# A two-layer gated attention and expert block: row transposes moved from TensorE to transposing transfers, and the batches interleaved in a new order

## The chip, the cores and the metric

The kernel runs on one core of one Trainium2 chip. The metric is the device time of one execution in microseconds (us), taken as the median of the runs. A core has a matmul engine (TensorE, PE in the profile, with its weight loads as PEld), three elementwise engines (VectorE or DVE, ScalarE or ACT, GpSimd or POOL), and SyncE (SP), which here only issues DMA transfers. Each engine works through its own list of instructions strictly in order and waits on semaphores that the other engines and the transfers raise.

## The reference, cut to what matters

The input is 32 batches of 256 tokens by 256 features, with 77 context rows a batch. Four residual steps follow each other, all of them on a layer norm of x:

```
x = x + tanh(g_xattn[0]) * L0_xattn(norm(x), ctx)   # relu projections, relu scores, mask, relu output
x = x + tanh(g_ffn[0])   * L0_ffn(norm(x))          # [x,-x] @ (+-1) 512x1024, relu, (+-1) 1024x1024, relu, (+-1) 1024x256
x = x + tanh(g_xattn[1]) * L1_xattn(norm(x), ctx)   # argmax of 77 scores picks memory rows; 16 heads, softmax over 77*; projection
x = x + tanh(g_ffn[1])   * L1_ffn(norm(x))          # 64 experts, 8 per token, capacity 128, and a shared expert
```

(*) In the kernel a memory row that is picked several times is one key with a count, so a token has 16 heads of 77 logits, 1232 probabilities in all, of which one row group (128 tokens, 8 heads) holds 616, padded to 640.

The layer norm and the softmax run along a token's row, while a matmul contracts over the partitions. So a norm (256 tokens by 256) has to be turned before the next projection, and so have the probabilities and the attention's output. Products that need more than 16 bits are split: a value is written as a high half in f16 and a low half (value minus high half, f16), and the matmul runs over both.

## The kernel before, in words

One batch is a chain of four stages, named in the code by the first letter of its steps: a (first attention), b (binary feed-forward: `b_l0`, `b_l1`, `b_l2`), c (second attention) and d (shared expert and routing). A hand-written `body(n)` on each engine interleaves them: it runs b of batch n, c of batch n-1, d of batch n-2 and a of batch n+1. The orders of the five engines are written out separately, and agree only by semaphores. Bodies 3 to 30 are a hardware loop, the others stand apart in front of and behind it. After all batches comes the expert phase: POOL has scattered every token's row into a table by expert (`scatter`, L647), SP loads 64 blocks of it (`load_rows`), and PE runs the experts.

**Turning a norm on PE.** ACT writes the norm in f32 (`ln_norm`, L817). PE transposes it by four 128x128 f32 transposes into PSUM (`transposes`, L1113, and `c_att`, L1294, for the attention's output). ACT copies the high half from PSUM (`tr_high`, L825) and DVE subtracts for the low half (`tr_low`, L1655). Norms 1, 2, 3 and the attention's output go this way: 16 transposes a batch. The four row groups of probabilities take five blocks each (`c_pt`, L1262 on PE, L896 on ACT, L1751 on DVE), 20 a batch.

**Turning a norm on SP.** Norm 0 already takes another way in all batches but the first two. POOL computes norm 0 and both halves as rows in f16, and one transposing DMA on SP (`turn_x`, L416) turns eight 128x128 f16 blocks from SBUF to SBUF.

**The feed-forward on PE.** `b_l0` (L1173) has four pieces of eight matmuls, into two PSUM banks in turn; piece j waits until piece j-2 was evicted, by ACT (`h_h`, L862) and then DVE (`h_l`, L1677). `b_l1` (L1189) has eight pieces of 16, `b_l2` (L1205) two of 16. DVE then adds the residual (`b_x2`, L1691), takes the statistics (L1626 to L1639), POOL the root (L690), DVE the shift (L1644), and ACT the norm.

**Other queues.** POOL copies x1 aside (`keep_x1`, L685) so that `x1` comes free. SP also loads x and the context, passes rows to the table's staging tile (`pass_rows`, L424), stores x4 and copies the queries into the stacked tile (`stack`, L430 and L433, eight transfers a batch). Near the end it loads the held weights of every fourth expert (`load_held`, 16 transfers of 384 KB).

## Time and profile before

| | |
|---|---|
| median of 2 runs | 1716.07 us (1713.07 and 1719.07) |
| span of the profiled execution | 1753.8 us |
| PE busy | 1618.4 us, 92% |
| DVE, ACT, POOL busy | 1345.8, 1049.5 and 1023.1 us |
| DMA in the whole span | 117.41 MB, 67 GB/s |

The profile follows one execution, and that one was longer than the timed runs: its span stands 37.7 us above the median. Differences are therefore worked out inside the profiled span and then set against the median. Busy shares are averages over set-up, the loop, the last batches and the expert phase; what a change in the loop is worth is read from windows inside it. A PE clock of 1.00 in a window means the higher of TensorE's two levels (2.4 GHz), 0.50 the lower one (1.2 GHz).

### The profile page before, as it was taken

How to read it: one execution, taken by the hardware profiler on the slowest of the kernel's cores; microseconds unless marked ns; L12 is line 12 of the kernel's file. 1: busy time of each engine (PE TensorE's matmuls, PEld its weight loads, DVE VectorE, ACT ScalarE, POOL GpSimd, SP SyncE). 2: the span in 40 equal slices, each digit the busy share in tenths (PEclk: the TensorE clock that was granted, in tenths of full speed). 3: DMA queues.
4: the chain of work that ended last, by engine and by line, in shares of the span. 5: the costliest groups of instructions: out<-in, count | busy, mean ns of one | idle time of the engine just before them, and what ended most of it. 6: DMA issues, size and time to landing. Idle time of an engine off the chain costs nothing.

```text
span 1753.8 us, 51499 instructions
## 1 busy us (share of the span) xinstructions
PE 1618.4 (92%) x16676; PEld 1417.6 (81%) x16676; DVE 1345.8 (77%) x4739; ACT 1049.5 (60%) x2917; POOL 1023.1 (58%) x1664
## 2 busy tenths in 40 slices
PE   5799999999999999999999999999999997578885
PEld 3688888888888888888888888888888886367774
DVE  6488888888788888888888888888888875546554
ACT  3466666666666666666666666666666654334442
POOL 4124666666566666666666666666666654455544
PEclk8899999999999999999999999999999998689998
DMA  7502211121111111111111111111111122258886
GB/s 225 170 22 65 59 55 52 55 58 46 34 37 36 45 33 52 37 28 38 41 37 37 37 33 33 33 34 37 29 37 33 31 63 78 94 126 204 188 198 126
DMA packets 146627, 117.41 MB, mean 67 GB/s; under 512 B 74656, under 2 KB 136042, under 8 KB 146585
## 3 DMA queue, kind: packets, MB, share of 16 engines
q1 hardware_dynamic: 112792, 97.71, 19.8%
q0 software_dynamic: 33792, 19.17, 6.2%
q8 instruction: 22, 0.36, 0.1%
q14 instruction: 21, 0.16, 0.0%
HBM read 51.63 MB, written 111.84 MB: 93 GB/s over the span
## 4 chain that ended last, share of the span: by engine, by line
PE 73%; DMA 9%; issue 6%; ACT 5%; DVE 4%; POOL 3%; another core or an unknown queue 1%; POOLq 0%; SPq 0%; ACTq 0%; DVEq 0%
PE bank L1189 21%; DMA out<-ey,aid 9%; PE bank L1087 9%; PE bank L1173 7%; PE ps_yo L1205 5%; PE ps_yo L1087 4%; PE ps_m L1087 4%; PE ps_lg L1087 4%; ACT p L890 3%; PE ps_tr L1113 3%; PE ps_yo L1262 2%; PE ps_m L1285 2%; PE ps_pt L1262 2%; PE ps_pt L1087 2%; PE ps_lg L1249 2%
## 5 line engine op out<-in xcount | busy, mean ns | idle before, releaser
L647 POOL DMA_INDIRECT table<-xs,slot x496 | 505.3, 1019 | 188.7 <-issue 168.6
L890 ACT ACTIVATE p<-ps_lg,rmax 128x77 f32<-128x77 f32 x1024 | 251.6, 347 | 78.9 <-DVE rmax L1745 78.3
L1189 PE MATMUL bank<-h_h,held 128*128 128x256 f16 x2048 | 266.6, 273 | 2.1 <-DVE h_l L1677 1.9
L1189 PE MATMUL bank<-h_l,held 128*128 128x256 f16 x2048 | 266.3, 273 | 0.0
L602 POOL TENSOR_TENSOR pool_pad<-pad_in 128x1 f32<-128x1 f32 x418 | 90.4, 216 | 284.2 <-PE ps_tr L1294 116.8
L1189 PEld LDWEIGHTS bank<-h_l,held 128*128 128x128 f16 x2048 | 200.8, 98 | 23.6
L1189 PEld LDWEIGHTS bank<-h_h,held 128*128 128x128 f16 x2048 | 195.3, 98 | 24.3 <-issue 1.8
L1677 DVE SCALAR_TENSOR_TENSOR h_l<-bank,h_h 128x512 f16<-128x512 f32 x256 | 173.0, 685 | 32.2 <-ACT h_h L867 13.8
L690 POOL TENSOR_TENSOR rs<-nt,minushalf 128x2 f32<-128x2 f32 x128 | 93.2, 728 | 126.1 <-DVE nt L1639 115.2
L867 ACT ACTIVATE h_h<-bank 128x512 f16<-128x512 f32 x128 | 77.1, 602 | 130.3 <-PE bank L1189 127.1
L784 POOL DMA_INDIRECT out<-ey,aid x64 | 98.6, 1541 | 96.7 <-DVE aid L2031 64.1
L1745 DVE TENSOR_REDUCE rmax<-ps_lg 128x4 f32<-128x308 f32 x256 | 119.2, 476 | 40.2 <-PE ps_lg L1249 32.5
L862 ACT ACTIVATE h_h<-bank 128x512 f16<-128x512 f32 x128 | 76.4, 597 | 86.6 <-PE bank L1173 85.5
L1205 PE MATMUL ps_yo<-held,h_h 128*128 128x256 f16 x512 | 117.4, 275 | 0.1
L1205 PE MATMUL ps_yo<-held,h_l 128*128 128x256 f16 x512 | 117.1, 272 | 0.0
L1173 PE MATMUL bank<-xt_h,held 128*128 128x256 f16 x512 | 100.2, 278 | 8.4 <-DVE dn_l L1571 5.9
L1626 DVE BATCH_NORM_STATS2 stats<-x 128x6 f32<-128x256 f32 x256 | 96.4, 418 | 10.9 <-DMA x<-in_x 0.7
L1087 PE MATMUL bank<-xt_h,gu_h 128*128 128x256 f16 x512 | 99.1, 276 | 5.5 <-DVE ac L1835 5.4
L1173 PE MATMUL bank<-xt_l,held 128*128 128x256 f16 x512 | 99.9, 277 | 0.0
L1087 PE MATMUL bank<-xt_l,gu_h 128*128 128x256 f16 x512 | 99.0, 276 | 0.0
L1087 PE MATMUL bank<-xt_h,gu_l 128*128 128x256 f16 x512 | 99.0, 276 | 0.0
L817 ACT ACTIVATE xn<-x,nb,rs 128x256 f32<-128x256 f32 x128 | 69.5, 591 | 39.2 <-DVE nb L1644 38.4
(275 smaller groups left out, 4520.2 us busy)
## 6 DMA issues: line engine op xcount, KB each, us to landing
ew<-in_e_wts SPq DMA_DIRECT2D x48, 384.0 KB
table<-xg SPq DMA_DIRECT2D x8, 1284.0 KB, 17.8
xg<-table SPq DMA_DIRECT2D x64, 160.5 KB
xs<-xr SPq DMA_DIRECT2D x31, 320.0 KB
x<-in_x SPq DMA_DIRECT2D x32, 256.0 KB
out<-x SPq DMA_DIRECT2D x32, 256.0 KB
table<-xs,slot POOLq DMA_INDIRECT x496
held<-in_e_wts SPq DMA_DIRECT2D x16, 384.0 KB
```

The lines of the kernel that those rows point to most:

```text
L602: return g.tensor_tensor(pool_pad[:, site:site + 1], pad_in[:, :], pad_in[:, :], ALU.mult)
L647: return g.indirect_dma_start(out=table, out_offset=bass.IndirectOffsetOnAxis(ap=slots[:, t, k:k + 1], axis=0), in_=rows[:, t, :], in_offs ...
L690: g.tensor_tensor(rs[i][:, :], nt[i][:, 0, :], minushalf[:, :], ALU.pow).then_inc(ln_root[i], 1)
L784: g.indirect_dma_start(out=out, out_offset=bass.IndirectOffsetOnAxis(ap=aid[u][:, 0:1], axis=0), in_=ey[u][:, :], in_offset=None, bounds_c ...
L890: ins = a.activation(p32[r % 2][:, h * S2:(h + 1) * S2], ps_lg[:, g_, h % HB * S2:(h % HB + 1) * S2], ACT.Exp, bias=rmax[r % 2][:, h:h + 1])
L1087: ins = mm(out_, s_, m_, start=(start and i == 0), stop=(stop and i == len(seq) - 1))
L1173: ins = mm(two(bank[j % 2])[:, m % 2, :], s_, m_, start=(k == 0), stop=(k == 3))
L1189: ins = mm(two(bank[j % 2])[:, m % 2, :], wb1[:, k, m * P:(m + 1) * P], hp[:, k, :], start=(i == 0 and k == 0), stop=(i == 1 and k == FK - 1))
L1205: ins = mm(two(ps_yo)[:, t, :], hp[:, k, t * P:(t + 1) * P], wb2[:, k, :], start=(i == 0 and k == 0), stop=(i == 1 and k == FK - 1))
L1626: last = v.bn_stats(stats[i][:, t, :], src[:, t, :])
L1677: v.scalar_tensor_tensor(hl[:, 2 * j:2 * j + 2, :], two(bank[j % 2]), 0.0, hh[:, 2 * j:2 * j + 2, :], ALU.max, ALU.subtract).then_inc(lo.s ...
L1745: v.tensor_reduce(rmax[r % 2][:, g_ * HB:(g_ + 1) * HB], ps_lg[:, g_, 0:HB * S2].rearrange("p (h k) -> p h k", k=S2), AX, ALU.max, negate= ...
```

## The change

**The turns.** All 36 transposes a batch leave PE. ACT now writes the high half of a norm or of the attention's output from the f32 rows into an f16 row tile (`high`), DVE the low half beside it (`low`), and SP turns both at once by a transposing DMA of eight blocks (`turn(i)`, i = 1 to 4) into the tile that the matmuls read. Probabilities go the same way in tiles of ten blocks (`c_phi` on ACT, `c_plo` on DVE, `turn_p(r)` on SP, r = 0 to 3). So SP issues eight more transposing DMAs a batch, beside the one of norm 0. Only the first two norms 0 stay on PE.

**PSUM and SBUF.** The tile that held turned probabilities now takes the a-stage; routing and its counts share another; the queries of the second attention go into `ps_yo`. The product tile `ac` has two buffers in place of four, and tiles of the expert phase lie over the loop's h tiles. POOL copies x2 aside as well (`keep_x2`, 128x512), and its scatters lose the waits that paced them.

**The order.** `body(n)` now spans four batches: `b_l0` and pieces 0 to 3 of `b_l1` of n, the rest of the feed-forward and the start of c of n-1, the rest of c and the start of d of n-2, the end of d of n-3. Three bodies (NB to NB+2) drain the pipeline.

The first place is the end of the feed-forward on PE. `ps_yo` is the output of `b_l2`, `bank` the two alternating banks, `ps_m<-vb,pt` the attention's values, `ps_m<-wc` its projection. Before, at the end of the loop body and its head:

```order
L1087 MATMUL bank<-xt_h,gu_l 128x256 x2
L1113 MATMUL ps_tr<-ident,xn 128x128 x2
...
L1173 MATMUL bank<-xt_h,held 128x256 x2
L1173 MATMUL bank<-xt_l,held 128x256 x2
...
L1087 MATMUL ps_m<-xt_h,wp_h 128x256 x2
```

With the change:

```order
L1257 MATMUL ps_yo<-held,h_l 128x256
...
L1326 MATMUL ps_m<-vb,pt 128x34 x3
L1326 MATMUL ps_m<-vb,pt 128x51 x3
...
L1223 MATMUL bank<-xt,held 128x256 x16
L1223 MATMUL bank<-xt,held 128x256 x8
...
L1149 MATMUL ps_m<-wc_h,xt 128x256 x2
...
L1149 MATMUL ps_yo<-xt,wp_h 128x256 x4
...
L1241 MATMUL bank<-h_h,held 128x256 x8
```

Before, pieces of the shared expert (`gu`) stood between the end of `b_l2` and the first `b_l0` of the next batch. Now only the last two row groups of the values stand there, and all four pieces of `b_l0` follow in one run.

The second place is ACT's list around the eviction of `b_l0` (`h_h<-bank`). Before, at the end of the body and its head:

```order
L817 ACTIVATE xn<-x,nb,rs 128x256 x2
L923 ACTIVATE ac_h<-ac 128x256
...
L918 ACTIVATE th<-bank 128x256
...
L825 ACTIVATE xt_h<-ps_tr 128x512
...
L862 ACTIVATE h_h<-bank 128x512
...
L871 ACTIVATE qp_h<-ps_m 128x512
```

With the change:

```order
L908 ACTIVATE rows_hl<-att 128x512
L894 ACTIVATE xn<-x,nb,rs 128x256 x2
L908 ACTIVATE rows_hl<-xn 128x512
L946 ACTIVATE h_h<-bank 128x512 x4
L955 ACTIVATE qp_h<-ps_yo 128x512
L894 ACTIVATE xr<-x,nb,rs 128x256 x2
L908 ACTIVATE rows_hl<-xr 128x512
L951 ACTIVATE h_h<-bank 128x512
```

The four evictions of `b_l0` now follow the high half of the attention's output and the whole of norm 2, which is made from the x2 that `b_l2` has just delivered.

The third place is SP's list. Before, one turn of the loop, and behind the last batch the end of the queue:

```order
L430 DMA qst<-qp_h 32x512 x4
L433 DMA qst<-qp_l 32x512 x4
L439 DMA out<-x 128x2x256
L416 DMA_TRANSPOSE xt<-xh 128x8x128
...
L424 DMA xs_z<-xr 128x2x320
L501 DMA held<-in_e_wts 128x768 x4
L531 DMA xg<-table 128x321 x2
L439 DMA out<-x 128x2x256
```

With the change:

```order
L470 DMA_TRANSPOSE pt<-p_hl 128x10x128
...
L497 DMA out<-x 128x2x256
...
L459 DMA_TRANSPOSE xt<-rows_hl 128x8x128 x3
...
L487 DMA qst<-qp_h 32x512 x4
L490 DMA qst<-qp_l 32x512 x4
L459 DMA_TRANSPOSE xt<-rows_hl 128x8x128
...
L481 DMA xs_z<-xr 128x2x320
L497 DMA out<-x 128x2x256
L572 DMA held<-in_e_wts 128x768 x4
L600 DMA xg<-table 128x321 x5
```

The store of the last batch (`out<-x`) and the last four held weights now both stand ahead of the first rows of the table (`xg<-table`).

The diff, cut to the new functions and the lines that set the order:

```diff
+            def turn(i, b):            # SP
...
+                sp.wait_ge(lo_ok[i], made)
...
+                sp.dma_start_transpose(xt[i][:, :, :, :, :].rearrange("p a t c n -> p (a t c) n"),
+                                       rows_hl[i][:, :, :, :].rearrange("p a t d -> p (a t d)")).then_inc(turned[i], 16)
+            def turn_p(r, b):          # SP
...
+                sp.dma_start_transpose(pt[r % 2][:, :, :, :].rearrange("p a k n -> p (a k) n"),
+                                       p_hl[r % 2][:, :, :].rearrange("p a n -> p (a n)")).then_inc(pt_in[r % 2], 16)
+            def high(i, b, src):       # ACT
...
+                w(act, turned[i], 16 * b)
+                a.activation(rows_hl[i][:, 0], src, ACT.Copy).then_inc(hi_ok[i], 1)
+            def c_phi(r, b):           # ACT
...
+                a.activation(p_hl[r % 2][:, 0, :], p32[r % 2][:, :], ACT.Copy).then_inc(p_hi.sem, 1)
+            def low(i, b, src):        # DVE
+                dve.wait_ge(hi_ok[i], b + 1)
+                v.tensor_tensor(rows_hl[i][:, 1], src, rows_hl[i][:, 0], ALU.subtract).then_inc(lo_ok[i], 1)
# SP, body(n), the second half
+                    store_x4(d)
+                    turn(1, m)
+                    turn(4, c)
+                    turn(2, n)
+                    stack(n)
+                    turn(3, c)
# PE, body(n), around b_l2
+                    c_av(1, d)
+                    b_l2(0, c)
+                    b_l2(1, c)
+                    c_av(2, d)
+                    c_av(3, d)
+                    b_l0(0, n)
...
+                    b_l0(3, n)
+                    c_wc(d)
+                    c_qp(c)
+                    b_l1(0, n)
# ACT, body(n), its head
+                    high(4, d, att[:, :, :])
+                    ln_norm(2, c, x2, xn[2])
+                    high(2, c, xn[2][:, :, :])
+                    b_l0(0, n)
...
# DVE, body(n), around b_x2
+                    low(1, n, xn[1][:, :, :])
+                    b_x2(c)
+                    c_norm(2, d)
+                    ln_sums(2, c, x2, x2_ok)
+                    ln_moments(2, c)
+                    c_norm(3, d)
+                    ln_shift(2, c)
+                    low(4, d, att[:, :, :])
+                    low(2, c, xn[2][:, :, :])
+                    b_l0(0, n)
```

(Conditions such as `if on(d):`, which drop a step where its batch does not exist, are left out between the lines.)

## Rows read from the trace of the kernel before

**Rows 1.** The page: span, and busy time, share and instructions of each engine.

```profile
span 1753.8 us, 51499 instructions
...
PE 1618.4 (92%) x16676; PEld 1417.6 (81%) x16676; DVE 1345.8 (77%) x4739; ACT 1049.5 (60%) x2917; POOL 1023.1 (58%) x1664
```

**Rows 2.** Windows, in the loop: us, busy by engine, PE clock, DMA share, GB/s.

```profile
375.00:420.00 45.00, 44.80 (x492) 39.72 (x491) 38.00 (x134) 29.88 (x84) 29.11 (x51) 1.00 0.20 58
```

**Rows 3.** Timeline of PE in the loop: start, length, instruction.

```profile
704.94 0.38 PE L1173 MATMUL bank<-xt_h,held 128*128 128x256 f16 x2
...
748.07 0.60 PE L1113 MATMUL ps_tr<-ident,xn 128*128 128x128 f32 x4
748.51 0.38 PE L1087 MATMUL bank<-xt_h,gu_h 128*128 128x256 f16 x2
...
749.82 0.38 PE L1173 MATMUL bank<-xt_h,held 128*128 128x256 f16 x2
...
750.69 0.38 PE L1087 MATMUL ps_m<-xt_h,wp_h 128*128 128x256 f16 x2
```

**Rows 4.** Timeline from the end of `b_l2` to norm 2.

```profile
743.34 0.38 PE L1087 MATMUL bank<-xt_h,gu_h 128*128 128x256 f16 x2
...
743.64 0.75 DVE L1691 SCALAR_TENSOR_TENSOR x<-ps_yo,sc,x_kept 128x512 f32<-128x512 f32 x1 [0.32 <-PE ps_yo L1205]
...
744.49 0.75 DVE L1626 BATCH_NORM_STATS2 stats<-x 128x6 f32<-128x256 f32 x2
...
745.89 0.72 POOL L690 TENSOR_TENSOR rs<-nt,minushalf 128x2 f32<-128x2 f32 x1 [0.27 <-issue]
...
746.64 0.16 DVE L1644 TENSOR_TENSOR nb<-nt,rs 128x2 f32<-128x2 f32 x1
...
746.87 1.08 ACT L817 ACTIVATE xn<-x,nb,rs 128x256 f32<-128x256 f32 x2
```

**Rows 5.** Lines of DVE, 300 to 1,200 us: busy, mean ns, idle before.

```profile
L1677 DVE SCALAR_TENSOR_TENSOR h_l<-bank,h_h 128x512 f16<-128x512 f32 x159 | 107.3, 685 | 9.6 <-ACT h_h L862 5.1 <-issue 3.7 <-ACT h_h L867 0.8
...
L1759 DVE TENSOR_TENSOR att<-ps_m,rden 128x128 f32<-128x128 f32 x80 | 23.3, 292 | 2.8
...
L1757 DVE RECIPROCAL rden<-ps_m 128x8 f32<-128x8 f32 x80 | 16.0, 200 | 7.4 <-PE ps_m L1285 7.4
```

**Rows 6.** Lines of ACT and of POOL, same stretch.

```profile
L825 ACT ACTIVATE xt_h<-ps_tr 128x512 f16<-128x512 f32 x59 | 35.1, 594 | 13.8 <-PE ps_tr L1113 12.3
...
L685 POOL COPY x_kept<-x 128x512 f32<-128x512 f32 x20 | 12.3, 613 | 0.0
```

**Rows 7.** Window of one batch, line 1285 (`c_av`) alone, four row groups: us, PE, PEld.

```profile
705.00:750.00 45.00, 2.15 (x60) 2.04 (x60) 1.00 0.14 36
```

**Rows 8.** Tiles `xt` and `qst`, 300 to 1,200 us: ns min/median/max to issue, us to landing.

```profile
L416 SPq DMA_TRANSPOSE xt<-xh x20: 1321/1332/1343, 316.6 to 1176.6; - x20
...
DMA to landing us min/median/max: 3.5/3.5/3.6
...
L430 SPq DMA_DIRECT2D qst<-qp_h x80: 507/582/593, 300.3 to 1162.4; - x80
```

**Rows 9.** Windows, and one row of PE's timeline, where PE works little.

```profile
1478.00:1480.00 2.00, 1.02 (x10) 0.67 (x7) 1.30 (x7) 0.61 (x2) 1.51 (x2) 1.00 0.06 9
1488.00:1490.00 2.00, 0.00 (x0) 0.00 (x0) 0.38 (x2) 0.00 (x0) 0.00 (x0) 0.50 0.02 0
74.00:76.00 2.00, 2.00 (x22) 1.75 (x21) 0.93 (x2) 1.19 (x2) 0.00 (x0) 0.91 0.02 5
...
69.52 0.40 PE L1173 MATMUL bank<-xt_h,held 128*128 128x256 f16 x1 [5.95 <-DVE dn_l L1571]
```

**Rows 10.** A window of the expert phase, and the group of the held weights among the DMAs.

```profile
1526.00:1528.00 2.00, 1.03 (x10) 0.68 (x7) 0.00 (x0) 0.00 (x0) 1.69 (x2) 1.00 1.00 333
...
held<-in_e_wts SPq DMA_DIRECT2D x16, 384.0 KB
```

More of the change, by code:

```diff
@@ L62, in w, with known @@
     eng.wait_ge(sem, value)
+def known(eng, *values):
+    for value in values:
+        if not isinstance(value, int):
+            eng.to_reg(value)
 class Many:
@@ L470, in _ @@
             load_x(1)
+            turn(1, 0)
             sp.wait_ge(bools_ok, 2)
@@ L1325, in d_gu @@
                     m = i * SK + j
-                    ins = three(two(bank[j % 2])[:, i, :],
+                    ins = three(four(bank[j % 2])[:, i],
                                 [(gu_h[:, c, m * P:(m + 1) * P], gu_l[:, c, m * P:(m + 1) * P], xt_h[3][:, c, :], xt_l[3][:, c, :]) for c in range(C2)])
@@ L1456, in second @@
-                if on(c):
-                    d_gu(3, c)
-            def body(n):
-                first(n)
-                second(n)
-            def last_batch(b):
-                c_av(3, b)
-                c_att(b)
-                c_wc(b)
-                transposes(3, b, xr)
-                d_route(b)
-                d_gu(0, b)
-                d_gu(1, b)
-                d_cp(b)
-                d_gu(2, b)
-                d_gu(3, b)
-                d_dn(0, b)
-                d_dn(1, b)
@@ L1876, in first @@
                     c_values(c)
-                if on(m) and on(n):
-                    ln_first(m)
+                if on(n):
+                    b_l1(0, n)
                 if on(c):
@@ L2009, in _ @@
             body(NB - 1)
-            first(NB)
-            last_batch(NB - 1)
+            body(NB)
+            body(NB + 1)
+            body(NB + 2)
             def match(e, u):
```

951 lines of the change are left out of this document (449 added, 502 removed).

## The prediction

> **What bounds the kernel now.** First read the page's line of busy shares [rows 1]: PE is busy 92% of the span, no other engine more than 77%. That is an average, so next come windows inside the loop. In one of 45 us PE is busy 44.80 us at a clock of 1.00, DVE 38.00, ACT 29.88, POOL 29.11, the DMA engines 0.20 of the time [rows 2]. The loop is bound by PE, and PE does not wait. Then PE's timeline: the same matmul of `b_l0` starts at 704.94 and at 749.82, so a batch takes 44.9 us [rows 3]. Whatever leaves PE shortens the loop, unless PE then waits; the question is whether the new order keeps it fed.
>
> **What leaves PE.** Four transposes stand between 748.07 and 748.51 [rows 3], so one costs 0.11 us, and 36 of them 36 x 0.11 = 4.0 us a batch. With no wait the period falls to 44.9 - 4.0 = 40.9 us.
>
> **What the new order adds: a wait at `b_l0`.** Piece 2 of `b_l0` needs bank 0, so piece 0 must be evicted, by ACT and then DVE. On ACT that eviction now stands behind norm 2, whose input x2 comes from the `b_l2` just finished; on DVE it stands behind both low halves. I follow this chain by its rows in the old loop [rows 4], where nothing waited for it. PE is free of `b_l2` at 743.34; x2 starts at 743.64 (+0.30) and its statistics at 744.49 (+0.85). The change puts `c_norm(2)` between them, a reciprocal of 0.20 and a product of 0.29 [rows 5]; I take +0.45. POOL's root starts 1.40 after the statistics, DVE's shift 0.75 after the root, ACT's norm 0.23 after that and it lasts 1.08 [rows 4]. The high half is a copy of 128x512, 0.60 by its twin [rows 6]; the low half is taken at 0.69, the price of the eviction of the same size [rows 5]. ACT's eviction of piece 0 (0.60) runs beside it, and DVE's follows with 0.69. Sum: 0.30 + 0.85 + 0.45 + 1.40 + 0.75 + 0.23 + 1.08 + 0.60 + 0.69 + 0.69 = 7.0 us from the end of `b_l2` to the start of piece 2.
>
> What has PE to do meanwhile? Two row groups of values: four take 2.15 us of PE [rows 7], 0.54 each with the tail of the last matmul, about 0.4 without. And pieces 0 and 1 of `b_l0`: one piece lasts from 749.82 to 750.69 = 0.87 [rows 3]. Together 2 x 0.4 + 2 x 0.87 = 2.5 us, so PE waits 7.0 - 2.5 = **4.5 us a batch**. Bounds: 3.4, if POOL and the handoffs answer at once (1.1 less in the chain); 6.1, if the last row group of probabilities lands late or POOL is inside a scatter (1.6 more). I take the middle, since every link has its own row.
>
> A second lane ends nearly there. `b_l0(0)` of the next batch needs turn 1. From the last piece of `b_l1`: eviction by ACT and DVE 0.60 + 0.69, the first statistics of another batch (`ln_first`) 1.3, taken from the 1.40 above, `c_norm(1)` 0.49, low half 0.69, transfer 3.5 [rows 8] = 7.3 us. PE has `c_av(1)`, `b_l2` (32 matmuls by 0.11) and two row groups: 0.4 + 3.5 + 0.8 = 4.7. So piece 0 would start 2.6 us late; with 0.87 for it and 1.29 for its eviction, piece 2 could start 4.8 us after its predecessors instead of 1.74. Even without norm 2 in the way PE would wait 3.0 us.
>
> **Turns on SP.** A turn of eight blocks is issued in 1.33 us and lands 3.5 us after its issue [rows 8]; it is 256 KB. One of ten blocks I take by size at 1.7 and 4.4, between 3.5 (no more than eight) and 4.4. Placed in strict series, each landing before the next issue, SP's list would be 5 x 3.5 + 4 x 4.4 + eight query copies of 0.58 [rows 8] + about 2 for four other issues = 41.7 us, below the new period; overlapped it is less. So SP is no bound, and the DMA engines, busy 0.20 [rows 2], have room. Now the rule that speaks against the change: the Trainium skill, "VectorE: DVE Perf Modes", section "The three transpose paths", gives 390 ns for a 128x128 bf16 transpose on TensorE and 1309 ns for one by the DMA, and "Rules for kernel authors" there says to use TensorE if a PSUM destination will do. By its figure as a rate, 80 blocks a batch would be an estimated 105 us, and the kernel some 3,500 us. The rows contradict it as a rate: eight blocks together land in 3.5 us, 0.44 each, and PE's transpose costs 0.11.
>
> **Other edits.** ACT and DVE do the same copies and subtractions from SBUF in place of PSUM: zero, between -0.1 and +0.1 each; both engines have over 5 us free in 45 [rows 2], and the links above carry what is on the path. `keep_x2` on POOL is 0.61 [rows 6] and is covered by POOL's 15 free us; uncovered, it would hold back x2 by as much. New waits elsewhere: `d_dn` behind `c_plo` and the last `ac`, `d_cp` behind routing's small DVE steps, `a_sv` behind its mask. They were covered by 1 to 3 us of matmuls; I take 0.5 together, bounds 0 and 1.6. On ACT and DVE everything queued behind an eviction waits with it, but PE is the one that waits last.
>
> **Sum.** Period 40.9 + 4.5 + 0.5 = 45.9, which is +1.0; 30 such periods, +30. The remaining two batches' worth of fill and drain loses 2 x 4.0 of transposes, of which I count -5. The drain runs the last batch nearly alone, and there four turns in a row are not covered: each 3.5 for 0.44 on PE plus about 0.3 of handoff, 2.8 more, +10. Behind the last store now stand four held weights of 384 KB and the store of 256 KB ahead of the first table rows: 1.8 MB at 333 GB/s [rows 10], 5.4 us, and about 2.5 to land, +8. Total +43: the profiled execution 1753.8 -> 1797, and the median, 37.7 below that span, 1716 -> **1759 us**.
>
> **The rivals.**
> - *Forecast (A), 0.47.* Periods of 45.0 to 47.1 with the 13 us at the edges: 1716 + 3 + 13 = 1732 at the low end (1730 rounded), 1716 + 66 + 13 = 1795 at the high one.
> - *Clock (B), slower still, 0.14.* PE then stands 4.5 us still in every batch. A window with PE busy 1.02 of 2 us stayed at 1.00, but one with no PE work was at 0.50; after a wait of 5.95 us one matmul lasted 0.40, more than two in a row at full clock (0.38), and 5 to 6 us later the clock was at 0.91 [rows 3, 9]. Losing half the speed for 5 us a batch is 2.4 us: 30 x 2.4 = 72 more, 1831. For it: the length of the wait. Against: PE has short work within it.
> - *Smaller wait (C), no measurable change, 0.22.* Norm 2 comes sooner and only turn 1's lane of 3.0 holds PE: periods of 43.4 to 44.9, 1684 to 1729.
> - *Fed PE (D), faster, 0.17.* The mechanism on the other side: PE runs out of step with the lists, so that x2, norm 2 and turn 1 are ready earlier than these rows say, and the stretch behind `b_l2` costs 1.5 us. It decides at a wait of about 2.4 us (period 43.3, 1716 - 48 + 13 = 1681). With 1.5: period 42.4, 1716 - 75 + 13 = 1654. For it: 4.0 us of PE work did go. Against: both lanes start only at `b_l1` and `b_l2` of the same body, and would both have to shrink.
> - *Transfers that are slow side by side (E), under 0.01.* If turns in flight together slow each other, SP's series passes the period and PE waits for turns. Were each landing doubled (7.0 and 8.8), the series would be 76.8 and the time 1716 + 30 x 31.9 + 13 = 2686. It decides from landings about an eighth longer than taken; against it stand 20 turns in the old loop that all landed in 3.5 to 3.6 beside other transfers [rows 8].
>
> What a measurement of this kernel can tell from no change is about 2%, 34 us: below 1682 is faster, above 1750 slower. Faster is D, 0.17. Same is C and the third of A up to 1750: 0.22 + 0.15 = 0.37. Slower is the rest of A and B: 0.32 + 0.14 = 0.46. The range of 8 in 10 runs from 1675, leaving out most of D, to 1831, leaving out half of B.
>
> **What would show it.** In the loop of the changed profile: no matmul of f32 128x128 outside the first batches; PE idle about 4 to 5 us a batch between `c_av(3)` and piece 2 of `b_l0`, with DVE's eviction `h_l` named as what ended it; ACT's first `h_h` behind two norm activations; a period near 45.9; PE busy near 41 of it. Turns of eight blocks landing in 3.5 us, of ten in about 4.4. The clock 1.00 in the loop, or below 1.00 if B holds. The prediction is wrong if PE waits less than 2.4 us there, or if its longest wait in a batch is for something else, a turn of probabilities above all.

## The result, and the profile after

The changed kernel takes 1806.3 us (1803.3 to 1809.3), the kernel before 1716.07: a ratio of 1.053, 95% interval 1.047 to 1.059. It is slower, by 90 us where the forecast said 43; it lies inside the range.

One thing has to be cleared first. The profile of before on which the prediction rests spans 1753.8 us; the same kernel profiled again (the first run below) spans 1715.1. The changed kernel's profile spans 1807.6. Against the first profile the change would seem to cost 53.8, against the second 92.5, and the medians say 90. So what follows compares with the second.

The page of the changed kernel, its span and engines (against [rows 1]):

```profile
span 1807.6 us, 50071 instructions
...
PE 1531.0 (85%) x15524; PEld 1311.1 (73%) x15524; DVE 1305.6 (72%) x4611; ACT 1026.0 (57%) x2789; POOL 1029.2 (57%) x1520
```

No engine is above 85%. Next, one window of 800 us in the loop, as in [rows 2]: us, then busy time (instructions) of PE, PE's weight loads, DVE, ACT and POOL, the granted clock, DMA share, GB/s. The changed kernel:

```profile
400.00:1200.00 800.00, 723.90 (x7786) 623.96 (x7784) 625.95 (x2213) 497.07 (x1365) 502.17 (x771) 0.97 0.42 88
```

The kernel before, profiled again:

```profile
400.00:1200.00 800.00, 794.85 (x8723) 706.49 (x8722) 674.52 (x2363) 533.12 (x1494) 516.47 (x890) 1.00 0.15 38
```

PE, which stood still 5 of 800 us, now stands still 76, and its clock has fallen from 1.00 to 0.97. The first piece of `b_l0` gives the period, as in [rows 3]; in the changed kernel, the second batch and the last:

```profile
87.68 0.61 PE L1223 MATMUL bank<-xt,held 128*128 128x256 f16 x2 [7.88 <-DMA xt<-rows_hl]
...
1477.80 0.94 PE L1223 MATMUL bank<-xt,held 128*128 128x256 f16 x7 [1.50 <-DMA xt<-rows_hl]
```

In the kernel before, profiled again, the same two pieces start at 68.62 and 1415.40. Thirty periods each: (1477.80 - 87.68) / 30 = 46.34 us against (1415.40 - 68.62) / 30 = 44.89. The difference of the spans splits at these rows and at the first expert (1611.78 and 1513.76):

| stretch | before, again | changed | difference |
|---|---|---|---|
| up to `b_l0` of the second batch | 68.6 | 87.7 | +19.1 |
| thirty periods | 1346.8 | 1390.1 | +43.3 |
| from the last `b_l0` to the first expert | 98.4 | 134.0 | +35.6 |
| experts to the end | 201.3 | 195.8 | -5.5 |

Per batch in the loop: PE was busy 794.85 / 800 x 44.89 = 44.60; less 36 transposes of 0.109 (3.92) that is 40.68. In the changed kernel it is busy 723.90 / 800 x 46.34 = 41.93, so 1.25 more for the same matmuls, of which some ran at the lower clock; and it stands still 4.41, before 0.29. Sum: -3.92 + 1.25 + 4.12 = +1.45.

What PE waits for in the same 800 us (17 batches): us in all, times, longest.

```profile
PE bank L1223 <- DMA xt<-rows_hl: 28.0, 17, 1.9
PE bank L1223 <- DVE h_l L1674: 23.0, 17, 3.6
PE ps_m L1326 <- DVE att L1757: 18.5, 18, 1.2
PE ps_m L1326 <- DMA pt<-p_hl: 3.3, 3, 1.3
```

Per batch that is 1.6 for turn 1, 1.4 for the eviction of `b_l0`'s first pieces, 1.1 for the attention's division (`c_norm`), 0.2 for turned probabilities. All but the last are between the row groups of `c_av` and the pieces of `b_l0`, around the place where the prediction put the wait. Batch by batch the wait for turn 1 is 1.5 to 1.9 and the one for the eviction 0.2 to 3.6; turn 1 is the longer one in 12 of the 17. Here is the chain of [rows 4] in the new order, in time order: start, length, instruction, idle time before it and what ended it. `b_l2` ended at 733.36.

```profile
733.67 0.74 DVE L1688 SCALAR_TENSOR_TENSOR x<-ps_yo,sc,x_kept 128x512 f32<-128x512 f32 x1
...
737.19 1.09 ACT L894 ACTIVATE xn<-x,nb,rs 128x256 f32<-128x256 f32 x2
737.25 2.94 PE L1223 MATMUL bank<-xt,held 128*128 128x256 f16 x16 [1.79 <-DMA xt<-rows_hl]
...
739.67 0.68 DVE L1674 SCALAR_TENSOR_TENSOR h_l<-bank,h_h 128x512 f16<-128x512 f32 x1
...
740.41 2.38 PE L1223 MATMUL bank<-xt,held 128*128 128x256 f16 x16 [0.22 <-DVE h_l L1674]
```

From 733.36 to piece 2 at 740.41 are 7.05 us; the prediction's sum of ten links was 7.0. Piece 0 started 1.79 late behind turn 1 (2.6 was forecast), and PE's wait for the eviction in this batch is only 0.22. The 16 matmuls of pieces 0 and 1 took 2.94, where two pieces at full clock take 1.74 by [rows 3] (1.92 with the tail of the last one). Windows of 2 us over the same stretch show why (first PE's busy time, and the clock as the third figure from the end):

```profile
735.00:737.00 2.00, 0.46 (x15) 0.35 (x15) 1.48 (x10) 0.38 (x1) 0.88 (x2) 1.00 0.75 149
737.00:739.00 2.00, 1.75 (x12) 1.37 (x13) 0.77 (x2) 1.89 (x5) 1.82 (x3) 0.74 0.02 0
739.00:741.00 2.00, 1.78 (x9) 0.94 (x8) 1.44 (x3) 1.11 (x3) 1.41 (x4) 0.50 0.68 132
741.00:743.00 2.00, 2.00 (x19) 1.72 (x17) 0.96 (x2) 0.77 (x2) 2.00 (x5) 0.90 0.74 131
```

PE stands mostly still up to 737 at a granted clock of 1.00; when it works again the clock drops to 0.50, the lower level of 1.2 GHz, and is back at 0.90 between 741 and 743. The loss lies in busy time, behind the wait. It does not come in every batch: of the 17 in the window, 7 have these 16 matmuls in 1.92, the other 10 in 2.7 to 3.5.

The turns themselves, against [rows 8]: tile `xt`, eight blocks, 69 turns in the window.

```profile
DMA to landing us min/median/max: 3.0/3.1/3.5
```

They land in 3.1 us, where 3.5 was taken from the loop before. A turn of probabilities (ten blocks) was put at 4.4. By the landing events of the trace three of the four land in a median of 3.3 to 3.4 us; the second, which is issued right behind a load, has a median of 3.8 and passes 5 us in 3 of 17 batches. One of those three, on the chain of waits (start, us, what):

```profile
723.42 5.39 DMA pt<-p_hl
728.89 0.75 ACT p_hl L981
```

SP issued the next batch's load of x (256 KB) 1.3 us before it, at 722.13. ACT's last piece of probabilities (piece 3, line 981) waits for that landing, 24.7 us in the 17 batches (0.6 to 4.0 each), and whatever stands behind it on ACT waits too.

### The profile page after: what moved, and what is told of

It is laid out like the page before. It is cut to its first block, busy times and chain, and to the rows that moved or that the text cites. A ratio compares the mean times of both kernels' runs of the same rounds, so it can differ in the third digit from the quotient of the medians.

```text
span 1807.6 us, 50071 instructions
## 1 busy us (share of the span) xinstructions
PE 1531.0 (85%) x15524; PEld 1311.1 (73%) x15524; DVE 1305.6 (72%) x4611; ACT 1026.0 (57%) x2789; POOL 1029.2 (57%) x1520
## 4 chain that ended last, share of the span: by engine, by line
PE 52%; DVE 14%; DMA 13%; issue 10%; ACT 5%; POOL 3%; SPq 2%; DVEq 1%; ACTq 0%; POOLq 0%
PE bank L1241 19%; PE bank L1149 6%; DMA out<-h_h,aid 6%; PE bank L1223 5%; PE ps_yo L1149 5%; PE ps_yo L1257 4%; DMA pt<-p_hl 3%; PE ps_pt L1149 3%; PE ps_m L1149 2%; PE ps_tr L1149 2%; DMA xt<-rows_hl 2%; POOL table L718 2%; ACT rows_hl L908 2%; DMA xg<-table 2%; DVE h_l L1674 2%
## 5 line engine op out<-in xcount | busy, mean ns | idle before, releaser
L718 POOL DMA_INDIRECT table<-xs,slot x496 | 523.1, 1055 | 200.7 <-issue 146.7
L1223 PE MATMUL bank<-xt,held 128*128 128x256 f16 x1024 | 166.7, 332 | 92.5 <-DMA xt<-rows_hl 56.4
L669 POOL TENSOR_TENSOR pool_pad<-pad_in 128x1 f32<-128x1 f32 x242 | 49.1, 203 | 309.6 <-DVE slot L1827 255.6
L1223 PEld LDWEIGHTS bank<-xt,held 128*128 128x128 f16 x1024 | 114.0, 117 | 138.3 <-DMA xt<-rows_hl 59.7
L1149 PE MATMUL bank<-xt,gu_h 128*128 128x256 f16 x1024 | 156.7, 277 | 11.8 <-DMA xt<-rows_hl 11.6
L860 POOL DMA_INDIRECT out<-h_h,aid x64 | 98.7, 1542 | 84.3 <-DVE aid L2012 60.2
L981 ACT ACTIVATE p_hl<-p 128x640 f16<-128x640 f32 x128 | 96.6, 755 | 53.6 <-DMA pt<-p_hl 53.5
L1149 PEld LDWEIGHTS bank<-xt,gu_h 128*128 128x128 f16 x1024 | 99.0, 99 | 29.9 <-DMA xt<-rows_hl 13.2
L1749 DVE TENSOR_TENSOR p_hl<-p,p_hl 128x640 f16<-128x640 f32 x128 | 105.0, 820 | 13.0 <-ACT p_hl L981 11.0
L1326 PE MATMUL ps_m<-vb,pt 128*128 128x34 f16 (+1 forms) x1920 | 69.5, 182 | 44.2 <-DVE att L1757 32.0
```

The lines of the kernel that those rows point to most:

```text
L718: return g.indirect_dma_start(out=table, out_offset=bass.IndirectOffsetOnAxis(ap=slots[:, t, k:k + 1], axis=0), in_=rows[:, t, :], in_offs ...
L860: g.indirect_dma_start(out=out, out_offset=bass.IndirectOffsetOnAxis(ap=aid[u][:, 0:1], axis=0), in_=ey[u][:, :], in_offset=None, bounds_c ...
L981: a.activation(p_hl[r % 2][:, 0, :], p32[r % 2][:, :], ACT.Copy).then_inc(p_hi.sem, 1)
L1149: ins = mm(out_, s_, m_, start=(start and i == 0), stop=(stop and i == len(seq) - 1))
L1223: ins = mm(four(bank[j % 2])[:, m % 2], s_, m_, start=(k == 0), stop=(k == 3))
L1749: v.tensor_tensor(p_hl[r % 2][:, 1, :], p32[r % 2][:, :], p_hl[r % 2][:, 0, :], ALU.subtract).then_inc(p_lo.sem, 1)
```

## The experiments

All against the kernel before, timed beside it (1717 to 1721 us). "Period" is measured as above.

**The kernel before, once more** (no edit).

> The kernel before, unchanged, profiled once more. In the profile of before the span was 1753.8 us and stood 37.7 above the median, while the changed kernel's span (1807.6) and median (1806.3) agree. Theory: that one execution lost time in places that are not a property of the kernel, first of all in the expert phase (212.9 us there, 195.8 in the changed kernel) and in batches longer than 44.9; a new execution has a span of 1712 to 1722, an expert phase of 195 to 200 and a mean batch below 45.0. Rival: the profile always adds about 38 us to this kernel; then the span is 1745 to 1760 again while the timed runs stay at 1716.

Measured: 1718.5 us, ratio 1.000 (0.999 to 1.001), span 1715.1, period 44.89, expert phase 201.3 (195 to 200 was expected). The rival is out: the offset of 37.7 between the first span and the median is no property of the kernel.

**The first statistics of the next batch moved behind the low half of the attention.**

```diff
 # DVE, body(n)
-                if on(m) and on(n):
+                if on(m) and on(n) and not on(d):
                     ln_first(m)
...
                     low(4, d, att[:, :, :])
+                if on(m) and on(n) and on(d):
+                    ln_first(m)
```

> The changed kernel with one DVE step moved: the first statistics of the next batch (ln_first, 1.3 us) go behind the attention's low half instead of ahead of c_norm(1) and the low half of norm 1, so turn 1 is issued about 1.3 us earlier. Theory (two lanes end together; piece 2 of b_l0 is bound by norm 2 on ACT and DVE): PE's wait for turn 1, 1.65 us a batch, falls to about 0.4, its wait for h_l grows by as much, the period stays at 46.3 (within 0.3), time 1797 to 1809. Rival (PE waits for the transfer, and norm 2 is hidden): the 1.3 us are gained, 30 x 1.3 = 39, time about 1767.

Measured: 1819.3, ratio 1.059 (1.056 to 1.061), period 46.63; both sides missed. PE's wait for turn 1 did not move (28.5 us over 17): in the trace norm 1 stood on ACT behind DVE's shift, and that behind the eviction of `b_l1`'s last piece, so `ln_first` had not been the late link.

**Piece 0 of `b_l0` evicted ahead of norm 2**, on ACT and on DVE.

```diff
 # ACT and DVE, body(n): b_l0(0, n) ahead of ln_norm(2) and of ln_shift(2)
+                    b_l0(0, n)
                     ln_norm(2, c, x2, xn[2])
                     high(2, c, xn[2][:, :, :])
-                    b_l0(0, n)
```

> The changed kernel with piece 0 of b_l0 evicted ahead of norm 2 on ACT and ahead of norm 2's low half on DVE. Theory (two lanes): piece 0 is itself late by turn 1, so its eviction ends only about 0.4 us sooner than now, and norm 2 ends 0.6 later; period 45.7 to 46.6, time 1785 to 1812. Rival (the order on ACT alone is the loss): the whole 1.35 us of waiting for h_l go and the clock recovers in part, 30 x 1.4 to 2.0 = 42 to 60, time 1746 to 1764.

Measured: 1829.8, ratio 1.066 (1.063 to 1.069), period 47.03. Neither side had that: the wait for the eviction stayed (25.1 us, now in 26 shares of at most 1.7), and norm 2 with all that hangs on it came later.

**The edges**: the first loads no longer wait for POOL's constants; the last store again behind the held weights, as before.

```diff
-                sp.wait_ge(consts2, 32)
+                if not isinstance(b, int) or b > 0:
+                    sp.wait_ge(consts2, 32)
...
-            body(NB + 1)
+            pass_rows(NB - 1)
...
+                if e == 1:
+                    store_x4(NB - 1)
```

> The changed kernel with both ends put back: the first load of x and of the context no longer waits for POOL's constants, and at the end the last four held weights are loaded ahead of the last store, which follows the second load of table rows. Theory: the first load is issued 6.0 us earlier (6.85 back to 0.8), and the first expert no longer waits 8 us behind the store and the weights; -14, time 1790 to 1796, loop period unchanged at 46.3. Rival for the start: set-up is bound by its weight loads, and the 6 us are hidden; then -8, 1798. Rival for the end: the first expert waits for the scatter of the last batch anyway; then -6, 1800.

Measured: 1802.5, ratio 1.049 (1.045 to 1.052); `b_l0` of the second batch at 82.3 (5.4 earlier), the first expert 10.0 earlier, but the expert phase 3.6 longer. The wait of the first expert, 9.2 in the changed kernel, is now:

```profile
PE ps_tr L1498 <- DMA xg<-table: 2.9, 1, 2.9
```

So both causes are there, 5.4 and 6.3 us; what is left of them is 6 us of span, not the 14 expected. The medians differ by 4 us only, which their intervals do not tell from none.

**PE kept busy while it waits for turn 1**: 14 matmuls of weights into a bank that is overwritten next.

```diff
-                    pe.wait_ge(turned[1], 16 * b + 16)
...
+                    if not isinstance(b, int):
+                        for k in range(14):
+                            mm(two(bank[0])[:, 0, :], wb1[:, k % FK, 0:P], wb1[:, k % FK, 0:S], start=True, stop=True)
+                    pe.wait_ge(turned[1], 16 * b + 16)
```

> The changed kernel with 14 idle matmuls of 128x256 (1.5 us at full clock) into bank 0 ahead of PE's wait for turn 1 in every loop body; their results are overwritten. It tells the low clock apart from the waits: in the changed kernel 16 matmuls of b_l0 behind the wait take 2.94 us where 1.74 would do, and PE is busy 41.9 us a batch where 40.7 would do. Theory (waits of 4.4 and a clock loss of 1.2 us a batch, the second caused by the first): the clock in the loop goes from 0.97 to 0.99 or 1.00, b_l0's 16 matmuls take 1.75, period 45.1 to 45.8, time 1770 to 1790. Rival 1 (the slow matmuls are hidden behind norm 2's lane): the clock rises, the period stays within 0.3 of 46.3, time 1797 to 1815. Rival 2 (the low clock has nothing to do with PE's wait): clock 0.97 as before, no gain.

Measured: 1792.5, ratio 1.043 (1.041 to 1.045), period 45.76: the theory's period, and a time 2.5 us above its range. Window and waits of this kernel:

```profile
400.00:1200.00 800.00, 739.83 (x8117) 644.11 (x8116) 633.77 (x2237) 501.15 (x1374) 508.84 (x786) 1.00 0.43 89
```

```profile
PE bank L1226 <- DVE h_l L1677: 34.5, 18, 3.7
```

The wait for turn 1 is filled (2.0 us left in the window), and the clock is back at 1.00, with work added. Less the 14 matmuls (1.53) PE is busy 40.8 a batch, close to the 40.68 worked out above: the 1.25 were the clock. But of the 1.25 us a batch that the matmuls had lost, only 0.57 came out of the period: the wait for the eviction grew by 11.5 us in the window. The clock cost is real, and more than half of it was hidden by the wait for the eviction.

**DVE's shift of norm 1 earlier**, ahead of the eviction of `b_l1`'s third piece.

```diff
+                if on(n) and past(n):
+                    ln_shift(1, n)
                 if on(c):
                     b_l1(2, c)
...
-                if on(n) and past(n):
-                    ln_shift(1, n)
```

> The changed kernel with DVE's shift for norm 1 ahead of the last two evictions of b_l1, so ACT's norm 1 need not wait for them: turn 1 comes about 1.2 us earlier (the earlier trial moved the wrong step: there ACT's norm 1 still ended at the same place). Theory (two lanes of nearly the same length): PE's wait for turn 1 falls from 1.65 to 0.3 to 0.6 us a batch, its wait for h_l grows by about 1, period within 0.4 of 46.3, time 1795 to 1815. Rival (turn 1 alone holds PE): 1.2 us gained, 1765 to 1775.

Measured: 1803.5, ratio 1.049 (1.047 to 1.052), period 46.10. The wait for turn 1 went from 28.0 to 25.4 us only; the low half still stood behind `ln_first` on DVE. The time is the theory's, but the wait did not fall as either side said, so it does not tell the two apart.

**Work put into the gap**: the down projection `d_dn` (24 matmuls, 2.6 us) moved from ahead of the last piece of `b_l1` to between `c_av(2)` and `c_av(3)`, with `d_x4` behind it on DVE, the store of x4 behind turn 2 on SP, and the waits that this order needs.

```diff
 # PE, body(n)
-                if on(e):
-                    d_dn(0, e)
-                    d_dn(1, e)
...
                     c_av(2, d)
+                    d_dn(0, e)
+                    d_dn(1, e)
                     c_av(3, d)
```

> The changed kernel with other PE work put into the gap: the 24 matmuls of the shared expert's down projection (2.6 us) stand between the last two row groups of values instead of ahead of the last piece of b_l1; x4 on DVE and its store on SP follow later in the body. No work is added or removed. Theory (the loop's loss is PE standing still behind b_l2 while norm 2 and turn 1 are made): idle falls from 4.4 to about 2 us a batch and the clock returns to 0.99 or more, period 42.5 to 43.7, time 1695 to 1735. Rival 1 (the loss is elsewhere: DMA transposes in flight slow the other engines or each other): period stays at 45.5 or more, 1780 and up. Rival 2 (the gap moves): c_av or c_lg now wait for probabilities, period 44.5 to 45.5, 1750 to 1780.

Measured: 1867.3, ratio 1.085 (1.082 to 1.088), period 48.15, far above the theory and the second rival. The first rival, transfers that slow the engines or each other, allows 1780 and more, but the traces speak against it: DVE's `h_l` takes a mean of 683 ns here and took 685 before [rows 5], and the turns of the changed kernel land in 3.1 us where 3.5 was usual. PE's waits:

```profile
PE bank L1224 <- DVE h_l L1681: 47.2, 16, 3.4
PE ps_m L1328 <- DMA pt<-p_hl: 25.6, 17, 3.3
```

The gap did not shrink, it moved. `d_dn` had been the cover of the second turn of probabilities: with it gone, PE reached `b_l2` only when ACT had waited for that turn. And the last row group of values now stood behind `d_dn`; its division on DVE and the high half of the attention on ACT come ahead of norm 2 in their lists, and so norm 2 was held up there as well (on the chain of waits `c_av(3)` starts at 772.54 and ACT's norm 2 at 774.14).

**That, the shift and the edges together.**

> The two steps moved (down projection into the gap, shift of norm 1 early) and both ends put back as in the run on the edges. Theory: on top of the run with the down projection alone, turn 1 is no longer late, 0.3 to 1.0 us a batch, and 4 to 10 us at the ends; time 1665 to 1715, at or below the kernel before (1717). Rival: with turn 1 earlier norm 2 alone holds PE and the ends give 4: 1690 to 1730.

Measured: 1883.5, ratio 1.095 (1.092 to 1.097), period 48.86, 2.5 us a batch more than the change. Both sides missed by far.

**The load of x on SP behind the second and third turn of probabilities**, in the changed kernel's order.

```diff
                 if on(d):
                     pass_rows(d)
-                if on(p) and not early(p):
-                    load_x(p)
                 if on(c):
                     turn_p(1, c)
                     turn_p(2, c)
+                load_x(p)
```

> The changed kernel with SP's load of x (256 KB) behind the turns of probabilities 1 and 2 instead of ahead of them. In the changed kernel turn 1 of the probabilities is issued 1.3 us behind that load and lands 5.4 us after its issue, while turns of eight blocks land in 3.2. Theory: the turn queues behind the load; it lands in 3.3 to 4.2, ACT's wait for it (1.6 us a batch ahead of c_phi(3)) falls below 0.6, and the period hardly moves (46.0 to 46.4) since PE's loss is behind b_l2, not here; time 1795 to 1808. Rival (the loop is bound by a chain through this turn): ACT's 1.0 to 1.6 us are gained, 30 x 1.0 to 1.6 = 30 to 48, time 1758 to 1776.

Measured: 1836.1, ratio 1.066 (1.064 to 1.069), period 47.21. ACT waits less for the turn (15.1 us for 24.7), but DVE now waits for x, 22.1 us in 17 batches, ahead of statistics that stand before other work in its list, and PE's wait for `att` rose from 18.5 to 30.5. Both sides missed. But PE as a whole does not stand still longer:

```profile
400.00:1200.00 800.00, 729.03 (x7694) 622.16 (x7692) 615.84 (x2190) 494.00 (x1357) 498.99 (x765) 0.95 0.41 87
```

Per batch that is 4.19 of stillness (4.41 in the changed kernel) and 43.02 of work (41.93), at a clock of 0.95. What this order loses, it loses in slower matmuls: the first 16 of `b_l0` take 2.9 to 3.6 us in 16 of 17 batches.

**Gap filled, every known late link moved**: `d_dn` in the gap, but now behind `c_av(3)`, the shift early, the load later, and piece 3 of the probabilities (`c_phi(3)` on ACT, `c_plo(3)` on DVE) behind an eviction of `b_l1` that does not wait for a turn.

> The down projection in the gap behind b_l2 once more (that trial ran at 1867), now without what stood in its way there: it comes behind the last row group of values, so norm 2 does not wait for it; ACT and DVE evict the last pieces of b_l1 ahead of the last probabilities, so b_l2 does not wait for a turn; the load of x comes behind the turns of probabilities 1 and 2; norm 1's shift comes early. Theory (the loss is PE's time behind b_l2, and the first trial only tied it to the turns of probabilities): idle falls from 4.4 to 1.5 to 2.5 us a batch, the clock to 0.98 to 1.00, period 43.0 to 44.5, time 1710 to 1755. Rival (the chain through the turns of probabilities is a bound of its own of about 46 us a batch): period 45.5 to 47.5, time 1780 to 1845, PE's waits at c_av for probabilities above 1 us a batch.

Measured: 1846.9, ratio 1.072 (1.069 to 1.074), period 47.71, just above the rival's range; DVE waits 31.6 us for x in the window, PE 42.2 for `att`.

**The same with the edges.**

> The same with both ends put back: first loads without the wait for POOL's constants, held weights ahead of the last store. Theory: 4 to 10 us less than the run without, 1703 to 1750; it would then stand within 2% of the kernel before (1717). Rival as in the run without: 1775 to 1840.

Measured: 1839.7, ratio 1.068 (1.066 to 1.071), period 47.72, as the rival had it: the edges again worth about 7 us.

**The same, and `ln_first` behind norm 2's low half**, so that DVE meets x late.

> The run with the gap filled and the edges put back (1840), with one step more: DVE's first statistics of the next x (ln_first) go behind the low half of the attention's output. In that run DVE stood 2.6 us in every batch waiting for x, whose load now follows the turns of probabilities, and c_norm(1), the low half of norm 1 and x2 were queued behind it. So here nothing of the four is in the way any more: norm 1, turn 1, the probabilities' turn and the load of x. Theory (several chains of nearly the same length end behind b_l2; each trial that shortened one alone left or lengthened another): with all of them out of the way piece 2 of b_l0 comes 7 us after b_l2 with 4.3 us of matmuls in between, period 43.4 to 45.0, time 1705 to 1765. Rival (DVE's list between the first logits and the last probabilities, 13 to 15 us that no trial shortened, closes a chain of its own): period 45.5 to 47, time 1770 to 1815.

Measured: 1818.0, ratio 1.057 (1.055 to 1.059), period 47.00, at the upper end of the rival's range (the time 3 us above it). PE's largest wait is now for probabilities:

```profile
PE ps_m L1332 <- DMA pt<-p_hl: 47.6, 30, 3.2
```

and the chain of waits shows the loop closing on itself (start, us, what; the lines left out are steps of DVE, ACT and PE in between):

```profile
733.02 4.87 DMA pt<-p_hl
...
738.63 4.16 PE ps_yo L1154 x24
...
760.96 0.48 DVE rmax L1754
...
777.25 1.34 SPq L472
778.91 0.41 SPq L430
779.58 0.38 SPq L437
780.14 4.71 DMA pt<-p_hl
```

From the issue of one last turn of probabilities to that of the next: its 4.87 to landing, PE's last row group of values, `d_dn` (the 24 matmuls) and `b_l0`, then PE's list up to the scores, 16 us of DVE's list from 760.96 on, and two loads issued on SP ahead of the next turn. 780.14 - 733.02 = 47.1: the period, with no engine full. The clock is part of this chain: the 24 matmuls of `d_dn` take 4.16 us behind PE's wait, at a clock of 0.64, where 2.6 is their price at 1.00.

**The two loads behind turn 1** on SP, nothing else of weight (`ln_first` late in one more batch); the edit is against the run before.

```diff
-                if on(p) and not early(p):
-                    load_x(p)
-                    load_ctx(p)
                 if on(c):
                     turn_p(3, c)
                 if on(m):
                     turn(1, m)
+                if on(p) and not early(p):
+                    load_x(p)
+                    load_ctx(p)
```

> The run with three lanes shortened, and one thing more: the loads of x and of the context of the next batch are issued on SP behind turn 1, no longer between the turns of probabilities. Theory (a closed chain through DVE's list and the last turn of probabilities, 47.0 us long, of which the load of x ahead of that turn is about 2.4): the last turn lands in 3.3 us after its issue and not 4.7, PE's waits for turned probabilities fall from 2.8 a batch to under 1, the period falls from 47.0 to about 44.6 and the time from 1818 to about 1746 (1730 to 1775). Rival (another chain of 46 to 47 us stands right behind it): PE's wait moves to the eviction at b_l2 or to the statistics that wait for x, the period stays at 46 to 47, 1790 to 1820.

Measured: 1774.8 (1772.6 to 1778.5), ratio 1.033 (1.031 to 1.035): 43 us less than the run before and 31 less than the change. Most periods are 44.8 to 45.3, the mean 45.66. The turn of ten blocks, and PE's waits for it:

```profile
DMA to landing us min/median/max: 3.3/3.4/4.2
```

```profile
PE ps_m L1332 <- DMA pt<-p_hl: 26.0, 28, 1.4
```

The theory said a landing of 3.3, waits for probabilities under 1 us a batch, a period of 44.6 and 1746 us. The landing is right, the wait halved (2.8 to 1.5), the time is at the end of its range. The chain through the load was real; right behind it stand others, and in the batch followed the chain of waits now runs through POOL's list of scatters, in which the roots of the norms stand. The windows of the run before and of this one:

```profile
400.00:1200.00 800.00, 718.19 (x7666) 617.00 (x7664) 615.34 (x2182) 490.34 (x1351) 498.27 (x762) 0.97 0.41 86
400.00:1200.00 800.00, 723.62 (x7905) 627.84 (x7903) 630.98 (x2243) 504.57 (x1391) 523.02 (x797) 0.99 0.41 88
```

Of the 1.34 us that the period lost, only 0.45 is PE's stillness; 0.9 is PE's work, 41.30 a batch for 42.20. Behind these shorter waits the clock stays up (0.99 in the window), and the first 16 matmuls of `b_l0` take 1.91 in all 17 batches.

**The order of the change kept** (`d_dn` in its place), everything beside the turns moved as in the run above but for the store of x4, which stays ahead of turn 1.

> The changed kernel with its order of PE's list kept (the down projection of the experts stays behind c_av(3)), and only what stands beside a turn moved: first loads free of the constants, the last store behind the held weights, the loads of x and of the context behind turn 1 on SP, ACT's third piece of probabilities behind the copy that doesn't wait for a turn, DVE's shift of norm 1 ahead of the low half. Theory: the turn of ten blocks lands in 3.3 us and not 5.4, ACT no longer waits 1.6 a batch for it, and PE's wait for turn 1 of 1.6 a batch is halved; period 45.0 to 45.8, and 12 us less at the edges: 1765 to 1795. Rival (chains of nearly equal length): period 46.3 unchanged, only the edges gained, 1800.

Measured: 1835.9, ratio 1.068 (1.067 to 1.070), period 47.50. Both sides missed. PE's waits in the window:

```profile
PE bank L1227 <- DMA xt<-rows_hl: 35.7, 17, 2.4
PE ps_m L1330 <- DMA pt<-p_hl: 26.4, 15, 2.0
PE bank L1227 <- DVE h_l L1678: 9.7, 12, 1.9
```

The wait for turn 1, which was to be halved, grew from 28.0 to 35.7, and the one for turned probabilities from 3.3 to 26.4; the wait for the eviction fell. PE's work, too, is 0.7 longer a batch than in the changed kernel, at a clock of 0.95. Against the run on the edges this kernel loses 33 us. Several moves differ between the two, and which of them costs it was not tried; the loads behind turn 1 are no gain by themselves.

## Why the prediction was wrong

*What left PE*: right. 36 f32 transposes a batch are gone; the run that keeps PE busy at a clock of 1.00 has 40.8 us of its old work a batch where it had 44.60, 3.8 for the 4.0 forecast.

*The wait at `b_l0`*: right in place and in the length of the chain, 7.0 us forecast from the end of `b_l2` to piece 2, 7.05 in the batch shown. Not right in what ends the wait: the prediction named the eviction and would be wrong by its own words if the longest wait of a batch was for something else. In 12 of 17 batches it is for turn 1, the second lane (2.6 late forecast, 1.8 measured), and three waits share the stretch. That the sum came out near (stillness of PE 4.5 + 0.5 = 5.0 a batch, measured 4.4) is in part luck: in the batch shown PE stands still 3.0 of the 7.05 and not 4.5, since its work there takes 4.0 at the lower clock and not 2.5, and 9.4 of the 23.0 us for the eviction fall into three batches with a late scatter on POOL (last section). Rivals C and D (a small wait, a fed PE) are out.

*The turns on SP*: right that they do not fill SP's queue (rival E is out; the loop's eight blocks land in 3.1). Ten blocks by size were put too high, 4.4 for a median of 3.3 to 3.8. Missed: the second turn of probabilities stands behind a load of 256 KB on the same queue, lands late in some batches (5.39 in the one shown), and ACT waits in line for it.

*The clock* was given to rival B alone, at 2.4 us a batch on top, with 0.14. It happened at half of that: 1.25 us more for the same matmuls. The run with matmuls in the wait shows that 0.57 of it, 17 us in thirty periods, is in the time. The argument against B, that PE has short work inside the wait, did not hold: in the batch shown PE worked 0.46 of the 2 us before the clock fell, and what followed ran slower.

*The period*: 45.9 forecast, 46.34 measured. Against 44.89 that is +43 for thirty, forecast +30. This is the smaller part of the miss. Within it the waits were put some 0.9 a batch too high (5.0 for the 4.12 that came on top), and the clock, at nothing in forecast A, 1.25 too low. (The range of periods, 45.0 to 47.1, is narrower than the prediction's own bounds on its waits give, 40.9 + 3.4 = 44.3 to 40.9 + 6.1 + 1.6 = 48.6; the measured one lies in both.)

*The failed step* is the sentence on "the remaining two batches' worth of fill and drain" with the terms behind it: -5, +10 (four times 2.8 are 11) and +8, 13 in all. Nothing was put for the fill but the transposes that it saves. Measured: +19.1, +35.6 and -5.5, 49 in all. That is 36 of the 49 us by which the sum was short.

Fill: the first `b_l0` starts at 46.49, before at 27.12, 19.4 late. In the changed kernel:

```profile
6.85 0.46 SPq L429 DMA_DIRECT2D x<-in_x  x1
...
34.77 0.75 DVE L1669 SCALAR_TENSOR_TENSOR x<-o,sc,x 128x512 f32<-128x512 f32 x1 [0.53 <-ACT o L940]
...
45.62 1.09 PE L1160 MATMUL ps_tr<-ident,xn 128*128 128x128 f32 x4 [11.51 <-POOL xn L779]
```

In the kernel before, again:

```profile
0.81 0.45 SPq L409 DMA_DIRECT2D x<-in_x  x1
...
20.76 0.74 DVE L1672 SCALAR_TENSOR_TENSOR x<-o,sc,x 128x512 f32<-128x512 f32 x1
...
27.12 0.61 PE L1173 MATMUL bank<-xt_h,held 128*128 128x256 f16 x2 [1.42 <-DVE xt_l L1655]
```

The first load is issued 6.0 later, since SP now waits for POOL's constants ahead of it. The prediction did not cost that; the run on the edges gave 5.4 back. x1 is 14.0 later, so some 8 more went between: in the changed kernel the first batch's queries stand behind its keys and wait for their copy (PE idle 4.7 there), where before they stood ahead of them. And from x1 to `b_l0` are 11.7 against 6.4: norm 1's turn is issued on SP at 40.80, and the second batch's rows, normalised on POOL, are turned on PE (45.62) ahead of `b_l0`. What went in behind the first load was read from the traces, not tried.

Drain: four uncovered turns were put at 2.8 each more, with the first expert's load at +8. From the last `b_l0` to the first expert, the changed kernel and then the kernel before, again:

```profile
1477.80:1611.78 133.98, 78.33 (x727) 61.53 (x728) 70.55 (x258) 51.27 (x143) 59.19 (x69) 0.76 0.45 113
1415.40:1513.76 98.36, 73.23 (x717) 59.22 (x715) 65.50 (x247) 46.31 (x139) 51.75 (x67) 0.83 0.26 84
```

PE stands still 55.7 us there, before 25.1; that is 30.5 of the +35.6. The rest is PE's work, 5.1 more although the transposes are gone, at a clock of 0.76 for 0.83. PE's waits in the last batch:

```profile
1573.85 0.61 PE L1149 MATMUL ps_m<-wc_h,xt 128*128 128x256 f16 x2 [5.31 <-DMA xt<-rows_hl]
1585.99 1.03 PE L1149 MATMUL bank<-xt,gu_h 128*128 128x256 f16 x4 [9.39 <-DMA xt<-rows_hl]
1611.78 0.66 PE L1494 MATMUL ps_tr<-ident,xg 128*128 128x128 f32 x2 [9.22 <-DMA xg<-table]
```

The +8 is 9.2, and 2.9 with the old order of the store and the weights. The turns are dearer than put: alone in the drain, a norm's turn costs its statistics, root, two halves and its landing in a row with nothing beside it, 9.39 where the longest wait for norm 3's rows in the same stretch before was 4.0. All of PE's waits for turns behind the last `b_l0` come to 25.0 us, against some 9 for norms and copies in the same places before; with the wait of the first expert (9.2, before 1.2) that makes 24 of the 30.5 us of stillness. These are waits read from the traces; of the drain only the first expert's was tried by a run. Why the expert phase is 5.5 us shorter was not taken apart.

Why did no edit bring the loop below 45? That PE is idle 4 us a batch says there is slack, and each run took away a wait that PE's list named. But another wait grew each time, or the matmuls became slower. One closed chain was followed all around, that of 47.1 us through the last turn of probabilities; that others of nearly the same length stand beside it (PE with norm 2, PE with norm 1 and turn 1) fits the waits that moved, but their lengths were not measured. And the clock goes with the order: for the same matmuls PE's work is 41.30 us a batch in the run with the loads behind turn 1 and 43.02 in the one with the load of x later, so that up to 1.7 us of what tells two orders apart is the speed of matmuls behind a wait, and not the wait. The best version of these, 1774.8, is still 3.3% slower than the kernel before. Whether an order exists that gets the 4.0 us back was not settled.

## What to carry to other kernels

A turn by transfer that replaces 0.44 us on PE (four transposes) took about 3 us to land here, plus both handoffs: free only where something else stands in the same place of the queues, and hardly in the fill and drain; cost those two stretches turn by turn, from the first instruction on. Where no engine is full, follow one chain from an event to the same event of the next batch: if that length is the period, moving the wait that the profile names longest can lengthen a second chain. Split every difference of periods into PE's stillness and PE's work: the second shows what the clock took. And profile the kernel before twice ahead of comparing spans.

## What the runs showed of the hardware

The kernel before has a stall of its own in every seventh batch. Two neighbouring batches, as windows:

```profile
383.01:427.48 44.47, 44.45 (x492) 39.59 (x489) 37.88 (x134) 29.94 (x85) 29.02 (x51) 1.00 0.17 49
427.48:476.00 48.52, 46.35 (x492) 40.40 (x489) 37.82 (x134) 29.93 (x85) 29.08 (x51) 0.96 0.14 35
```

and where the second loses its time:

```profile
461.45 1.01 POOL L647 DMA_INDIRECT table<-xs,slot  x1 [2.85 <-issue]
...
465.48 1.18 PE L1113 MATMUL ps_tr<-ident,xr 128*128 128x128 f32 x4 [2.15 <-ACT xr L817]
```

One scatter starts 2.85 us late (0.3 to 0.5 is usual), the norm's root behind it is late, PE stands still 2.15 us, and in the 5 us from 465.48 on the clock is at 0.66: the batch is 4.05 longer, of which 1.9 is slower matmuls. It recurs in the batches that start at 742.80 and 1056.58, and in the run with the loads last every seventh batch too (49.70 for 45.16). The changed kernel has it as well:

```profile
492.95 0.98 POOL L718 DMA_INDIRECT table<-xs,slot  x1 [3.87 <-issue]
...
509.29 2.10 PE L1223 MATMUL bank<-xt,held 128*128 128x256 f16 x9 [3.64 <-DVE h_l L1674]
```

Again at 818.70 and 1146.11: the three longest waits for the eviction (3.6, 3.6 and 2.2) follow these scatters. They come some 316 us apart before and 326 in the changed kernel, seven batches in each, so they go by batches and not by time. What holds the scatter is open.
